# Delta-rule layer: the head-wise normalisation of the output moved from ScalarE to GpSimd

## The chip, the core and the metric

The kernel runs on one core of one Trainium2 chip. A core has five engines with queues of their own: TensorE (PE, its weight loads listed apart as PEld), VectorE (DVE), ScalarE (ACT), GpSimd (POOL) and SyncE (SP, which here only issues DMAs). They meet through semaphores alone. The metric is the device time of one execution in microseconds (us), as the median of several runs.

## The reference, cut to what matters

Two transformer-like layers over x of shape (8, 512, 128): layer 0 with attention and a capped mixture of experts, layer 1 with a gated delta rule and another mixture of experts. The change lies in the delta rule (8 batches, 512 tokens, 16 value heads, head size 64):

```python
def step(S, xs):
    q_t, k_t, v_t, g_t, b_t = xs
    S = S * jnp.exp(g_t)[..., None, None]
    kv = jnp.einsum('bhk,bhkv->bhv', k_t, S)
    S = S + jnp.einsum('bhk,bhv->bhkv', k_t, (v_t - kv) * b_t[..., None])
    o_t = jnp.einsum('bhk,bhkv->bhv', q_t, S)
    return (S, o_t)
...
var = jnp.mean(o * o, axis=-1, keepdims=True)
o = o * jax.lax.rsqrt(var + EPS) * norm_w * jax.nn.silu(z)
return o.reshape(b_, t_, V_DIM) @ W_out
```

What the change touches is the last product but one: o times its inverse norm (one number for each token and head), and then times the gate silu(z).

## The kernel before

`network` runs four stages with a barrier between them: `setup`, layer 0, `delta1` (the delta rule) and `experts1`. All that follows is in `delta1`.

**Tiling.** The recurrence is taken in chunks of CK = 32 tokens. The 8 batches are two groups of four; the four batches of a group lie side by side on the 128 partitions, 32 tokens each. Each group has NCK = 16 chunks, so there are NS = 32 steps, k = 0 to 31, with one group behind the other. Steps come in pairs m = k // 2; a step is called even or odd by k. A step works in two halves f = 0 and 1 of 8 heads (512 columns) each. Every engine has its own hand-written program, a loop over k that calls small functions, so the order on an engine is the order of the calls. Semaphore counts (`half(k, f)`, `done(kind, x)`) tie them together.

**The recurrence in a step.** TensorE reads the state (`read_out`, L2514: keys times S into the banks BK, queries times S into BQ). VectorE scales the first (`read_out`, L2010, writes Xs). GpSimd subtracts it from the values (`residual`, L1917) and decays the state (`decay`, L1929: S times GC, 128x1024, one for each half). TensorE solves the triangular system (`solve`, L2548), ScalarE copies the result (`weights`, L2319, writes Ws), GpSimd weighs it (`weigh`, L1938: Ud = Ws times dl, with dl broadcast along the head), TensorE forms the state's increment (`add_state`, L2565), and VectorE subtracts it from S (`update`, L2111). After `update(k, 1)` TensorE may do `read_out(k + 1)`.

**The output in a step.** ScalarE writes O from the bank with a decay (`decayed`, L2259), VectorE subtracts the part within the chunk (`accumulate`, L2117). In the next step ScalarE squares and sums O for each head (`square_out`, L2249, into nrm), VectorE and ScalarE turn the sums into inverse norms (`total` L2018 and L2019, `root_out` L2269, `inverse_norm` L2024 and L2025, semaphore `v_rn`). Then `normed` on ScalarE (L2326) multiplies O by nrm, head by head: 16 activations of 128x64 with a per-partition scale. `gated` on GpSimd (L1945) multiplies O by the gate zs, one instruction of 128x512 for each half. TensorE transposes O (`turned`, L2588), ScalarE copies it out (L2339), and one step later TensorE multiplies by the output weights (`output`, L2595).

**What stands behind `normed` on ScalarE.** `keys(k + 1)` copies the transposed keys to Kt (L2333), `gate(k, 0)` and `gate(k, 1)` compute zs (L2313; each waits until `gated` of the step before has read the old zs of its half), and then the copies of `turned`. TensorE's second gate product (`gate(k, 1)`, L2484) takes the bank that `keys` has to empty, and TensorE's queue is in order: behind it stand, in odd steps, the norms of keys and queries (`norms`, L2457), then `turned`, two projections (L2475), `output` and `read_out(k + 1)`.

**VectorE's fill work.** Beside the recurrence VectorE convolves (`conv`, L2057, with its sum in PSUM), builds the decay matrices in even steps (`norms` L2041 to L2047, `attend` L2071 to L2082, `turn` L2086), and inverts the triangular matrices by substitution (`substitute`, L2095 and L2096, 30 rounds of two dependent tensor_tensor instructions for each pair of steps, with all operands in SBUF). Rounds 1 to 5 stand between `update(k, 0)` and `accumulate(k, 1)` of the even step, 6 to 11 behind its `update(k, 1)`; the odd step has the rest, 18 to 23 between its two updates. The first round waits for GpSimd (`initial`, L1963 to L1968).

**GpSimd's order in a step**: `window` (copies of the layer's input), `residual` x2, `decay(k, 0)`, in even steps `diag` (L1911), `weigh` x2 and `initial`, then `decay(k, 1)`, `gated(k - 1)`, `halo`.

Of the kernel before, what the change touches and what calls it, by code (L numbers as in the profile page):

```python
# [7 lines left out]
ALU = mybir.AluOpType  # L8
ACT = mybir.ActivationFunctionType
# [23 lines left out]
HV, HK, DK = 16, 8, 64  # L33
# [1732 lines left out]
def delta1(nc, g, a, w):  # L1766
# [7 lines left out]
    with Stage(nc, ["p_ks", "p_qs", "p_w", "p_ds", "p_pu", "p_kk", "p_m",  # L1774
                    "v_ks", "a_qs", "v_s", "v_o", "v_lt", "v_at", "v_ac", "v_tt", "v_conv", "v_by", "v_ss",
                    "v_rn", "v_rk", "p_nm", "p_nt", "a_rt", "v_link", "g_x", "g_s", "g_d1", "g_t", "g_t0", "g_halo", "g_on", "g_hw", "g_ac", "v_nm", "a_kq", "g_ud",
                    "a_m", "a_w", "a_on", "a_sq", "a_osq", "a_or", "d_al0", "d_al1", "d_out",
                    "k_y0", "k_y1", "k_y2", "k_y3", "k_m", "k_x", "k_v", "k_var", "k_rstd", "k_nm", "k_xn", "k_xT", "k_hT",
                    "k_rows", "k_be", "k_e", "k_ee", "k_al", "k_alz", "k_ad", "k_ga", "k_gb", "k_gce"]) as s:
        raw = s.sb("raw", [P, 4, 2, 4, KS - 1 + 2 * CK])  # L1780
# [68 lines left out]
        with nc.Block() as block:  # L1849
# [40 lines left out]
            def _(pool):  # L1890
# [48 lines left out]
                                    ALU.mult).then_inc(s["g_ud"], 1)  # L1939

                def gated(k):
                    for f in range(2):
                        pool.wait_ge(s["a_m"], done("z", 2 * k + f))
                        pool.wait_ge(s["a_on"], half(k, f))
                        G.tensor_tensor(O[:, k % 2, f, :], O[:, k % 2, f, :], zs[:, f, :], ALU.mult)\  # L1945
                            .then_inc(s["g_on"], 1)

# [289 lines left out]
            def _(act):  # L2237
                A_ = nc.scalar.activation

                def square_out(k, f):  # L2240
                    act.wait_ge(s["v_o"], half(k, f))
                    if half(k, f) > 1:
                        act.wait_ge(s["a_osq"], half(k, f) - 1)
                    if k >= 2:
                        act.wait_ge(s["a_on"], half(k - 2, 1))
                    for h in range(HF):
                        of = slice(DK * h, DK * h + DK)
                        at = HF * f + h
                        last = A_(osq[:, of], O[:, k % 2, f, of], ACT.Square, accum_out=nrm[:, k % 2, at:at + 1])  # L2249
                    last.then_inc(s["a_osq"], 1)  # L2250
# [64 lines left out]
                def weights(k, f):  # L2315
# [1 line left out]
                    if k:  # L2317
                        act.wait_ge(s["p_pu"], half(k - 1, f))
                    A_(Ws[:, f, :], BK[f][:, :], ACT.Copy).then_inc(s["a_w"], 1)  # L2319

                def normed(k):
                    act.wait_ge(s["v_rn"], k + 1)
                    for f in range(2):
                        for h in range(HF):
                            of = O[:, k % 2, f, DK * h:DK * h + DK]
                            last = A_(of, of, ACT.Copy, scale=nrm[:, k % 2, HF * f + h:HF * f + h + 1])  # L2326
                        last.then_inc(s["a_on"], 1)

                def keys(k):
                    act.wait_ge(s["p_m"], done("kt", k))  # L2330
# [53 lines left out]
                for k in range(FIRST, LAST):  # L2384
                    here, past = 0 <= k < NS, 0 <= k - 1 < NS
                    if past:
                        square_out(k - 1, 0)
                    if (k + 4) // 2 < NP:
                        project(2 * (k + 4))
                    if k == FIRST:  # L2390
                        act.wait_ge(s["k_e"], 2)
                        A_(sy, sy, ACT.Exp).then_inc(s["k_ee"], 1)
                    if 0 <= k - 2 < NS:
                        output(k - 2)
                    if past:
                        square_out(k - 1, 1)
                    if here:
                        decayed(k, 0)
                        decayed(k, 1)
                    if here and k % 2 == 1:  # L2400
                        weights(k, 0)
                    if (k + 4) // 2 < NP:
                        project(2 * (k + 4) + 1)
                    if here and k % 2 == 0:
                        weights(k, 0)
                    if past:
                        root_out(k - 1)
                    if 0 <= k + 1 < NS:
                        values(k + 1, 0)
                    if here:  # L2410
                        weights(k, 1)
                    if (k + 4) // 2 < NP:
                        squash(2 * (k + 4))
                        squash(2 * (k + 4) + 1)
                    if k == FIRST + 1:
                        act.wait_ge(s["k_e"], 3)
                        A_(al, sp, ACT.Exp, scale=w["nA"][:, 0:1]).then_inc(s["k_al"], 1)
                    if k == -1:
                        for x in range(4):
                            last_decays(x)  # L2420
                    if 0 <= k + 1 < NS:
                        values(k + 1, 1)
                    if past:
                        normed(k - 1)
                    if 0 <= k + 1 < NS:
                        keys(k + 1)
                    if here:
                        gate(k, 0)
                        gate(k, 1)
                    if k % 2 == 1 and 0 <= k // 2 + 2 < NP:  # L2430
                        root(k // 2 + 2)
                    if past:
                        turned(k - 1, 0)
                        turned(k - 1, 1)
# [270 lines left out]
```

## Time and profile before

| | |
|---|---|
| median of 3 runs | 2621.98 us (2610.21 to 2622.99) |
| the profiled execution's own time | 2618.09 us |
| its span in the trace | 2616.3 us |
| busy, whole span | PE 2091.7, DVE 1826.4, ACT 1477.8, POOL 791.8 us |
| the 32 steps of the delta rule | from 1152.9 us to some 2190 us |
| instructions of `normed` | 512, 331 to 348 ns each |
| instructions of `gated` | 64, 1260 to 1482 ns each |
| instructions of `weigh`, 1250 to 2150 us | 54, 1038 to 1280 ns, median 1042 |

A row of a timeline is a start in us from the span's start, a duration in us, engine, line, operation, output<-inputs and a count; neighbours of one kind on one engine are merged. In brackets stands how long the engine sat idle before and what released it. An instruction's duration contains any time for which it was held up after its start. Instructions of one engine can overlap by some 0.1 us.

### The profile page before, as it was taken

What the parts mean: (1) busy time and instruction counts of PE and PEld (TensorE: products, weight loads), DVE (VectorE), ACT (ScalarE), POOL (GpSimd) and SP (SyncE); (2) the same over time, 40 slices, a digit from 0 to 9 for tenths busy, and PEclk for the clock granted to TensorE, in tenths of its full rate; (3) what the DMA queues carried; (4) which work ended last, traced back from release to release, by engine and by line L of the source; (5) the groups of instructions that cost most, each with busy time, mean ns of one, the idle gap of its engine ahead of it and who ended that gap; (6) DMA issues with size and microseconds to landing.
All of it is one profiled execution on the core that took longest, in us unless ns stands there. A gap on an engine that the chain in (4) does not pass through costs nothing. (4 is left out here: it accounts for less than half of the span.)

```text
span 2616.3 us, 64390 instructions
## 1 busy us (share of the span) xinstructions
PE 2091.7 (80%) x25432; PEld 1286.1 (49%) x25432; DVE 1826.4 (70%) x4473; ACT 1477.8 (56%) x4029; POOL 791.8 (30%) x852
## 2 busy tenths in 40 slices
PE   2698988988888584578888888888888884777984
PEld 1244444444444363245555555556555553455652
DVE  2477777777776434688899999899998863673333
ACT  0267677677676321546777777777776663222221
POOL 1000001001001134034444444444444442104884
PEclk9599999999998887788999999999999896797997
DMA  5100000000000062100000000000000003334334
GB/s 184 41 1 1 9 5 9 5 5 9 5 5 9 13 178 62 24 18 12 13 13 13 13 13 13 13 13 13 13 13 5 5 6 102 81 98 99 44 45 88
DMA packets 109533, 85.58 MB, mean 33 GB/s; under 512 B 22366, under 2 KB 97282, under 8 KB 108976
## 3 DMA queue, kind: packets, MB, share of 16 engines
q1 hardware_dynamic: 95664, 68.31, 8.9%
q0 software_dynamic: 13568, 13.14, 3.1%
q8 instruction: 202, 3.31, 0.5%
q14 instruction: 99, 0.81, 0.1%
HBM read 59.22 MB, written 22.71 MB: 31 GB/s over the span
## 5 line engine op out<-in xcount | busy, mean ns | idle before, releaser
L624 ACT ACTIVATE Pr<-Pr,nmax 128x512 f32<-128x512 f32 x512 | 341.3, 715 | 173.4 <-DVE nmax L555 170.7
L729 PE MATMUL bank<-ident,Pr 128*128 128x128 f32 x2048 | 301.5, 289 | 82.5 <-DVE PT L564 65.7
L729 PEld LDWEIGHTS bank<-ident,Pr 128*128 128x128 f32 x2048 | 231.9, 147 | 254.8 <-DVE PT L564 165.8
L555 DVE CUSTOM_DVE_ANT_0 Pr<-bank,Tb 128x512 f32<-128x512 f32 x512 | 330.9, 684 | 22.8 <-PE bank L715 20.7
L564 DVE COPY PT<-bank 128x512 f32<-128x512 f32 x256 | 176.5, 690 | 176.3 <-PE bank L743 171.7
L2491 PE MATMUL bank<-Wcv,hw 128*128 128x512 f32 x512 | 241.1, 615 | 4.3 <-ACT bank L2282 3.4
L2095 DVE TENSOR_TENSOR pr<-AC,Tc 128x30 f32<-128x30 f32 (+14 forms) x480 | 218.8, 456 | 33.1 <-POOL Tc L1968 19.3
L2096 DVE TENSOR_TENSOR Tc<-Tc,pr 128x30 f32<-128x30 f32 (+14 forms) x480 | 199.2, 415 | 16.5
L631 ACT ACTIVATE PT<-bank 128x512 f32<-128x512 f32 x256 | 150.7, 589 | 71.6 <-PE bank L743 66.8
L715 PE MATMUL bank<-kp,qp 8*128 8x512 f32 x1024 | 172.6, 663 | 0.8 <-DVE nmax L555 0.8
L1917 POOL TENSOR_TENSOR Xs<-vt,Xs 128x512 f32<-128x512 f32 x64 | 80.8, 1274 | 277.2 <-DVE Xs L2010 276.1
L433 POOL DMA_INDIRECT disp<-H,slot x32 | 31.8, 994 | 402.2 <-DVE slot L504 394.9
L2491 PEld LDWEIGHTS bank<-Wcv,hw 128*128 128x128 f32 x512 | 95.5, 194 | 108.2 <-issue 97.7
L743 PE MATMUL bank<-PT,vp 128*9 128x512 f32 x1024 | 145.8, 640 | 0.0
L2326 ACT ACTIVATE O<-O,nrm 128x64 f32<-128x64 f32 x512 | 125.3, 334 | 2.8 <-DVE nrm L2025 2.8
L2484 PE MATMUL bank<-Wz,hw 128*128 128x512 f32 x128 | 81.4, 723 | 53.6 <-ACT Kt L2333 33.3
L424 POOL TENSOR_SCALAR H<-X,rs,nm 128x128 f32<-128x128 f32 x32 | 13.9, 448 | 361.4 <-DVE nm L543 361.4
L2249 ACT ACTIVATE osq<-O 128x64 f32<-128x64 f32 x512 | 122.9, 250 | 0.0
L2057 DVE SCALAR_TENSOR_TENSOR bank<-raw,cwq,bank 128x256 f32<-128x256 f32 x256 | 111.8, 483 | 4.6 <-ACT bank L2282 1.8
L1929 POOL TENSOR_TENSOR S<-S,GC 128x1024 f32<-128x1024 f32 x60 | 115.0, 1916 | 0.0
L1596 POOL DMA_INDIRECT acc<-eo,ids x64 | 100.9, 1577 | 43.7 <-DVE eo L1731 19.9
L1945 POOL TENSOR_TENSOR O<-O,zs 128x512 f32<-128x512 f32 x64 | 82.2, 1293 | 102.2 <-ACT O L2326 102.2
(407 smaller groups left out, 4437.5 us busy)
## 6 DMA issues: line engine op xcount, KB each, us to landing
aB<-alpha SPq DMA_DIRECT2D x64, 128.0 KB, 2.8
Tb<-scores SPq DMA_DIRECT2D x1, 7168.0 KB
w<-in_L_ffn_W SPq DMA_DIRECT2D x16, 256.0 KB, 5.4
rawW<-in_L_ffn_up_w SPq DMA_DIRECT2D x16, 256.0 KB, 3.1
rawW<-in_L_ffn_gw SPq DMA_DIRECT2D x16, 256.0 KB, 3.5
rawW<-in_L_ffn_down_w SPq DMA_DIRECT2D x16, 256.0 KB, 4.0
disp<-zero SPq DMA_DIRECT2D x1, 2580.0 KB, 14.7
xin<-disp SPq DMA_DIRECT2D x8, 322.5 KB, 6.1
```

The costliest lines, as they stand in the source:

```text
L555: V.tensor_tensor_reduce(out=Pr[:, s, i, :], in0=pS[hh][:, :], in1=Tb[:, h, at:at + L], scale=-1.0, scalar=3.0e38, op0=ALU.add, op1=ALU.mi ...
L564: V.tensor_copy(PT[:, m % NPS, :], pT[m % 2][:, :]).then_inc(r["b_evd"], 1)
L624: A_(Pr[:, s, i, :], Pr[:, s, i, :], ACT.Exp, scale=-1.0, bias=nmax[:, s, i:i + 1])\
L631: A_(PT[:, m % NPS, :], pT[m % 2][:, :], ACT.Copy).then_inc(r["b_eva"], 1)
L715: mm(pS[hh][:, :], qp[rows, G % SLOTS, i * P:(i + 1) * P], kp[rows, G % SLOTS, :], start=True, stop=True, tile_position=(32 * hh, 0)).then ...
L729: last = TR(pT[m % 2][:, t * P:(t + 1) * P], Pr[:, (G % 2) * HG + hh, t, j * P:(j + 1) * P], ident[:, :])
L743: mm(pO[32 * hh:32 * hh + HD0 + 1, :], vp[:, b % 2, j, G % NG * HG + hh, :], PT[:, m % NPS, :], start=(j == 0), stop=(j == LT - 1), tile_p ...
L2095: link(V.tensor_tensor(o, bcast(AC[:, i + 1:CK, i], 2, i), bcast(Tc[:, i, 0:i], 1, n), ALU.mult))
L2096: link(V.tensor_tensor(Tc[:, i + 1:CK, 0:i], Tc[:, i + 1:CK, 0:i], o, ALU.add))
L2249: last = A_(osq[:, of], O[:, k % 2, f, of], ACT.Square, accum_out=nrm[:, k % 2, at:at + 1])
L2326: last = A_(of, of, ACT.Copy, scale=nrm[:, k % 2, HF * f + h:HF * f + h + 1])
L2491: last = mm(o[:, :], tokens(k, i), Wcv[:, i, 512 * f:512 * f + 512], start=(i == 0), stop=(i == KS - 1))
```

## The change

`normed` on ScalarE is gone, with its 16 activations a step. `gated(k)` on GpSimd first waits for the inverse norms (`v_rn`), multiplies each half of O by nrm, broadcast along the head (two instructions of 128x512), and then multiplies by the gate as before (two instructions). The semaphore `a_on` becomes `g_nrm`, which GpSimd raises; ScalarE's `square_out` waits on it where it waited on `a_on`. Nothing else is changed: VectorE's and TensorE's programs are the same.

```diff
 def gated(k):
+    pool.wait_ge(s["v_rn"], k + 1)
+    for f in range(2):
+        G.tensor_tensor(hd(O[:, k % 2, f, :]), hd(O[:, k % 2, f, :]),
+                        bcast(nrm[:, k % 2, HF * f:HF * f + HF], 2, DK), ALU.mult)\
+            .then_inc(s["g_nrm"], 1)
     for f in range(2):
         pool.wait_ge(s["a_m"], done("z", 2 * k + f))
-        pool.wait_ge(s["a_on"], half(k, f))
+        pool.wait_ge(s["g_nrm"], half(k, f))
         G.tensor_tensor(O[:, k % 2, f, :], O[:, k % 2, f, :], zs[:, f, :], ALU.mult)\
             .then_inc(s["g_on"], 1)
...
 def square_out(k, f):
...
     if k >= 2:
-        act.wait_ge(s["a_on"], half(k - 2, 1))
+        act.wait_ge(s["g_nrm"], half(k - 2, 1))
...
-def normed(k):
-    act.wait_ge(s["v_rn"], k + 1)
-    for f in range(2):
-        for h in range(HF):
-            of = O[:, k % 2, f, DK * h:DK * h + DK]
-            last = A_(of, of, ACT.Copy, scale=nrm[:, k % 2, HF * f + h:HF * f + h + 1])
-        last.then_inc(s["a_on"], 1)
...
     if 0 <= k + 1 < NS:
         values(k + 1, 1)
-    if past:
-        normed(k - 1)
     if 0 <= k + 1 < NS:
         keys(k + 1)
```

GpSimd in the last part of an even step and the first of the odd step behind it, before:

```order
L1963 TENSOR_TENSOR AC<-AC,rkT 128x1024
L1965 AFFINE_SELECT Tc<-AC 128x1024
L1968 MEMSET Tc 128x32
L1929 TENSOR_TENSOR S<-S,GC 128x1024
L1945 TENSOR_TENSOR O<-O,zs 128x512 x2
L1956 COPY raw<-raw 128x8x3 x2
L1904 COPY hw<-hTa 128x128 x4
L1917 TENSOR_TENSOR Xs<-vt,Xs 128x512 x2
```

The same place with the change:

```order
L1968 TENSOR_TENSOR AC<-AC,rkT 128x1024
L1970 AFFINE_SELECT Tc<-AC 128x1024
L1973 MEMSET Tc 128x32
L1929 TENSOR_TENSOR S<-S,GC 128x1024
L1944 TENSOR_TENSOR O<-O,nrm 128x512 x2
L1950 TENSOR_TENSOR O<-O,zs 128x512 x2
L1961 COPY raw<-raw 128x8x3 x2
L1904 COPY hw<-hTa 128x128 x4
L1917 TENSOR_TENSOR Xs<-vt,Xs 128x512 x2
```

The two products with nrm stand between the second decay of the state and the products with the gate; all else keeps its order (line numbers behind L1941 are higher by 5).

## Rows read from the trace of the kernel before

**Rows 1.** The page, part 1: busy us, share of the span, instructions.

```profile
PE 2091.7 (80%) x25432; PEld 1286.1 (49%) x25432; DVE 1826.4 (70%) x4473; ACT 1477.8 (56%) x4029; POOL 791.8 (30%) x852
```

**Rows 2.** VectorE's waits, 1250 to 2150 us: us in total, times, longest.

```profile
DVE Xs L2010 <- PE bank L2514: 28.4, 26, 3.5
...
DVE S L2111 <- PE bank L2565: 12.1, 15, 4.0
```

**Rows 3.** Busy time by stretch: length, five engines, PEclk: steps 11, 12, 25.

```profile
1514.60:1546.50 31.90, 27.11 (x437) 16.32 (x439) 28.97 (x65) 22.81 (x74) 12.91 (x14) 0.95 0.01 2
1546.50:1579.40 32.90, 30.65 (x726) 21.95 (x719) 29.43 (x59) 25.23 (x108) 17.53 (x19) 0.95 0.10 23
1966.00:2000.80 34.80, 28.72 (x434) 16.80 (x436) 31.32 (x65) 22.34 (x72) 12.70 (x14) 0.85 0.01 2
```

**Rows 4.** Group by form, 1250 to 2150 us: busy us, mean ns, idle before.

```profile
L1938 POOL TENSOR_TENSOR Ud<-Ws,dl 128x512 f32<-128x512 f32 x54 | 58.5, 1083 | 88.3 <-ACT Ws L2319 88.3
```

**Rows 5.** Timeline, last half of step 11 (odd): ACT, PE, POOL, DVE.

```profile
1530.39 3.91 ACT L2326 ACTIVATE O<-O,nrm 128x64 f32<-128x64 f32 x16
...
1534.84 1.13 PE L2484 MATMUL bank<-Wz,hw 128*128 128x512 f32 x2 [2.13 <-ACT Kt L2333]
...
1545.31 1.95 PE L2514 MATMUL bank<-S,kq 64*32 64x128 f32 x76
...
1526.71 1.90 POOL L1929 TENSOR_TENSOR S<-S,GC 128x1024 f32<-128x1024 f32 x1
1532.54 1.37 POOL L1945 TENSOR_TENSOR O<-O,zs 128x512 f32<-128x512 f32 x1 [3.93 <-ACT O L2326]
...
1528.79 0.17 DVE L2025 TENSOR_TENSOR nrm<-nrm,rkq 128x16 f32<-128x16 f32 x1
...
1529.48 1.28 DVE L2111 TENSOR_TENSOR S<-S,bank 128x512 f32<-128x512 f32 x2
...
1546.46 0.69 DVE L2010 TENSOR_TENSOR Xs<-bank,gk 128x512 f32<-128x512 f32 x1 [1.40 <-PE bank L2514]
```

**Rows 6.** Timeline, last third of step 12 (even): POOL, DVE, ACT, PE.

```profile
1566.38 1.90 POOL L1929 TENSOR_TENSOR S<-S,GC 128x1024 f32<-128x1024 f32 x1
1568.24 2.48 POOL L1945 TENSOR_TENSOR O<-O,zs 128x512 f32<-128x512 f32 x2
...
1569.60 1.20 DVE L2095 TENSOR_TENSOR pr<-AC,Tc 128x58 f32<-128x58 f32 x1
1570.83 0.25 DVE L2096 TENSOR_TENSOR Tc<-Tc,pr 128x58 f32<-128x58 f32 x1
...
1569.59 0.60 ACT L2313 ACTIVATE zs<-bank 128x512 f32<-128x512 f32 x1 [2.06 <-POOL O L1945]
...
1575.65 1.62 PE L2514 MATMUL bank<-S,kq 64*32 64x128 f32 x52
```

**Rows 7.** Timeline, start of step 12 (even), VectorE.

```profile
1547.82 0.69 DVE L2010 TENSOR_TENSOR Xs<-bank,gk 128x512 f32<-128x512 f32 x1 [0.67 <-PE bank L2514]
...
1548.52 0.19 DVE L2042 TENSOR_TENSOR gk<-gT,rkq 128x32 f32<-128x32 f32 x1
1548.62 1.26 DVE L2043 COPY rkd<-rkq 128x32 f32<-128x32 f32 x1
...
1552.92 1.22 DVE L2071 TENSOR_TENSOR_SCAN Lt<-aB,Lt 128x512 f32<-128x512 f32 x1
```

**Rows 8.** Timeline, start of step 0, VectorE.

```profile
1152.90 0.63 DVE L2010 TENSOR_TENSOR Xs<-bank,gk 128x512 f32<-128x512 f32 x1
1153.96 0.69 DVE L2010 TENSOR_TENSOR Xs<-bank,gk 128x512 f32<-128x512 f32 x1 [0.43 <-PE bank L2514]
...
1154.87 1.30 DVE L2042 TENSOR_TENSOR gk<-gT,rkq 128x32 f32<-128x32 f32 x1
1156.10 1.92 DVE L2043 COPY rkd<-rkq 128x32 f32<-128x32 f32 x1
...
1160.77 1.22 DVE L2071 TENSOR_TENSOR_SCAN Lt<-aB,Lt 128x512 f32<-128x512 f32 x1
```

More of the change, by code:

```diff
@@ L1776, in delta1 @@
                     "v_rn", "v_rk", "p_nm", "p_nt", "a_rt", "v_link", "g_x", "g_s", "g_d1", "g_t", "g_t0", "g_halo", "g_on", "g_hw", "g_ac", "v_nm", "a_kq", "g_ud",
-                    "a_m", "a_w", "a_on", "a_sq", "a_osq", "a_or", "d_al0", "d_al1", "d_out",
+                    "a_m", "a_w", "g_nrm", "a_sq", "a_osq", "a_or", "d_al0", "d_al1", "d_out",
                     "k_y0", "k_y1", "k_y2", "k_y3", "k_m", "k_x", "k_v", "k_var", "k_rstd", "k_nm", "k_xn", "k_xT", "k_hT",
```

## The prediction, made blind

> **What bounds the kernel now.** The page's first part [rows 1] shows TensorE at 80% and VectorE at 70% of the span, ScalarE at 56%, GpSimd at 30%. That speaks for moving work from ScalarE to GpSimd, but it is an average over four stages. So I cut the delta rule into steps with the table of stretches [rows 3]. An odd step (11) takes 31.9 us with VectorE busy for 29.0, the even one behind it (12) 32.9 with 29.4; ScalarE is busy for 22.8 and 25.2. The stage has 32 such steps, and a barrier behind it, so what it loses or gains shows in the total.
>
> The table of waits [rows 2] says what VectorE lacks: in 900 us (28 steps) 28.4 us for TensorE's read-out of the state and 12.1 for the state's increment, its largest waits beside that for GpSimd's first matrix, which the change doesn't touch. VectorE sets the pace, and TensorE's late read-out adds about 2 us to each pair of steps. In the timeline of step 11 [rows 5] that lateness begins at the line that the change removes: 3.91 us of `normed`, then TensorE's second gate product idle for 2.13 us until Kt is copied, and 12 us later VectorE idle for 1.40 us until the read-out. The second L2010 waits for another 0.67 us [rows 7]. So the removed work is on a path that costs something, in odd steps. In the even step the relief can't help: the read-out started at 1575.65 [rows 6], and VectorE came to it only at 1579.4 [rows 3].
>
> The third view is VectorE's own durations, and it decides. In step 12 [rows 6] L2095 with 58 columns takes 1.20 us and its partner L2096 with 58 columns 0.25 us. The first lies beside GpSimd's products with the gate (1568.24 to 1570.72), the second behind them.  So a VectorE instruction with both inputs in SBUF is held until the GpSimd instruction beside it ends. The state's update L2111, which has one input in PSUM, takes 1.28 us for two [rows 5], 0.64 each for 512 columns, with nothing added. VectorE's busy time has these holds in it.
>
> The Trainium skill ("SBUF — State Buffer", section "Who interferes with whom") states this as a rule against such a move: a VectorE instruction with two SBUF inputs contends with a GpSimd instruction that reads SBUF, one with at most one doesn't, and the loser blocks fully. The rows just named agree (1.20 against 0.25 us). Were the page's lock paid for the whole of every added instruction, wherever it lies, the result would be the second rival below.
>
> **The change part by part.** Per step, ScalarE loses 16 activations (3.91 us in step 11). GpSimd gains two broadcast products of 128x512. The nearest row is `weigh`, the same form: mean 1083 ns [rows 4], of which some 1.05 is its length when nothing holds it. Two make 2.1 us. GpSimd has room in sum (12.9 and 17.5 busy of 32 us [rows 3]), so only the place matters.
>
> *Odd steps, relief.* `keys` no longer waits behind `normed`, so TensorE's second gate product starts up to 2.13 us sooner, and all behind it (norms, transposes, projection, output, read-out). VectorE's wait of 1.40 us before the first L2010 goes. The waits for the read-out are 28.4 us; 14 of the second L2010 by 0.67 are 9.4 of these, so the first ones are 19, about 1.4 for each odd step: **-19 us**.
>
> *Odd steps, cost.* The inverse norms are ready at 1528.96 and GpSimd is free then (its decay ended at 1528.61) [rows 5]. The two new products would run to 1531.1. Beside them VectorE has `accumulate` and `update(k, 0)`, up to 1530.76 [rows 5], with their PSUM inputs, which aren't held; only the next L2095 is, for some 0.3 us. The gate products still hold two substitution instructions, as they do now. **+4 us** for 14 steps.
>
> *Even steps, end.* Here GpSimd is late: after Tc it has `decay(k, 1)` (1566.38 to 1568.28) and then the gate products back to back [rows 6]. The inverse norms were ready long before, so the new products go in between, and five GpSimd instructions in a row stand where three did. VectorE is in rounds 1 to 5, whose instructions take some 0.25 us free [rows 6], and gets one through for each GpSimd instruction. Two more are held: 2 x (1.05 - 0.25) = 1.6 us, ahead of `update(k, 1)`, on which the next step waits. 14 steps (2 to 28): **+22 us**. Nothing hides it: VectorE doesn't wait at the odd step's start.
>
> *Even steps, start.* This term is the least obvious. In step 12 the second L2010 comes 1.36 us behind the first, since the read-out is late [rows 5, 7]; L2041 and L2042 then slip between GpSimd's two `residual` instructions (0.19 us) and L2043 is held by the second (1.26). In step 0 the read-out was less late (0.43 in place of 0.67), the second L2010 came 1.06 us behind the first, and the pattern is another: L2042 held for 1.30 us by the second `residual` and L2043 for 1.92 by the decay [rows 8]. From the first L2010 to the scan L2071 step 0 needs 7.87 us, step 12 6.46; step 0 has no L2018 and L2019 (0.28 us). So a read-out that comes 0.3 us sooner costs 1.7 us. With the relief of 2.13 us against waits of 1.40 the second L2010 won't wait, and step 0's pattern becomes that of the even steps. Between 0 and 1.7 I take 1.7, since step 0 shows it, for 12 of 14 steps (behind step 15, which has no update, and at one other the read-out stays late): **+20 us**. The 0.67 us of waiting is inside this figure.
>
> *The rest.* With VectorE later, L2111's small waits in even steps go (0.2 us each): **-3**. Behind the last step `normed` and the second gate product in series are 3.9 + 1.3 = 5.2 us, four products 4.6. Steps 30 and 31, where VectorE has little to do, may gain some 1 us each: with these **-2.5**.
>
> *A cover.* In even steps zs and the transposes wait for the gate products (the 2.06 us of L2313 [rows 6]), so the new 2.1 us delay TensorE as well, and with the start's 1.7 the read-out begins some 4 us later in the step. Now it begins 3.75 us ahead of VectorE's L2010 (1575.65 against 1579.4) and needs 1.15 of these (1545.31 to 1546.46 in step 11 [rows 5]). VectorE itself is later by 3.3. Hidden, with some 2 us to spare.
>
> Sum: -19 + 4 + 22 + 20 - 3 - 2.5 = +21.5. Against the profiled execution's 2618.1 us that is 2639.6. The median of 2622 is 4 above this execution; the three runs spread over 13 us. I say **2640 us**.
>
> **The rivals.**
>
> *Relief wins (faster).* The decisive point is whether VectorE is held by the new products at the even step's end. If TensorE's and ScalarE's queues are what paces that end (zs waits 2.06 us there), or if GpSimd's products don't hold these short instructions, and the start pattern stays as in step 12, only the relief is left: -19 - 9 for the second L2010, -3, -2.5, and some for zs: 2585 us. For it: 3.9 us a step leave a queue behind which TensorE waits. Against: 1.20 against 0.25 [rows 6].
>
> *Every added instruction is paid in full (slower still).* If VectorE's phase shifts so that the new products meet substitution in odd steps too, 62 x 1.05 = 65 us of holds replace the 26 above: 2679 us. Against: the `v_rn` that releases them comes right ahead of the PSUM work in VectorE's own order.
>
> *The start pattern stays (no change).* Without the +20: 2618 + 1.5 = 2620 us. This needs the read-out to stay as late as now, for instance since the clock is lower.
>
> *The clock (slower).* Step 25 takes 34.8 us against step 11's 31.9, with the granted clock at 0.85 in place of 0.95 [rows 3]: stretches at 1.2 in place of 2.4 GHz behind idle time of TensorE. The even steps get more idle time (2 us ahead of the transposes), the odd ones less. Should a third of the odd steps more go that way: +3 x 5 = 15 on the forecast, 2655 us; the other way round, -3 x 3 = -9 on it.
>
> **How the numbers follow.** Forecast 2640: 0.5. Clock above it: 0.1. Start pattern stays: 0.22. Relief wins: 0.1. Paid in full: 0.08. The range takes in all but the relief's centre and the full price: 2606 to 2668. A measurement tells about 0.5% from no change, 13 us, so faster is below 2609, slower above 2635: faster 0.11, same 0.3 (the pattern case and the forecast's lower edge), slower 0.59.
>
> **What would show it.** Right, if in the trace after: (1) even steps last 35 to 36 us and odd ones near 31; (2) L2010's waits for the read-out in odd-to-even turns are gone; (3) L2043 takes 1.9 us in even steps, with the scan about 8.1 us behind the first L2010; (4) five GpSimd instructions in a row at the even step's end with five VectorE ones of 1 to 1.9 us beside them; (5) in odd steps the new products lie beside L2117 and L2111 of unchanged length. Wrong, if VectorE waits at the start of odd steps (TensorE has become late there, the cover is gone), if L2043 is still at 1.26 us (the start term falls), or if the substitution's mean time is as before (the holds fall).

## The result, and the profile after

| | before | after |
|---|---|---|
| median of 4 runs each | 2620.07 us (2610.21 to 2622.99) | 2644.20 us (2643.39 to 2647.32) |
| the profiled execution | 2618.09 us | 2647.32 us |
| span in the trace | 2616.3 us | 2645.5 us |

The changed kernel is slower: the ratio is 1.0107, with a 95% interval of 1.0078 to 1.0135. The forecast was 2640 us.

ScalarE has lost 116 us of busy time and GpSimd has gained 68 (against [rows 1]); VectorE, whose program is the same, has gained 54:

```profile
PE 2086.5 (79%) x25432; PEld 1296.6 (49%) x25432; DVE 1880.7 (71%) x4473; ACT 1361.8 (51%) x3517; POOL 859.9 (33%) x916
```

VectorE's waits from 1250 to 2150 us (us in total, times, longest). The read-out, 28.4 us in [rows 2], is down to 0.2:

```profile
DVE S L2116 <- PE bank L2560: 4.8, 4, 2.5
...
DVE Xs L2015 <- PE bank L2509: 0.2, 1, 0.2
```

So the wait went as forecast, and VectorE's own instructions became longer. Steps 11, 12 and 25, with the columns of [rows 3]:

```profile
1533.20:1565.10 31.90, 30.00 (x570) 19.83 (x561) 30.39 (x65) 23.76 (x87) 14.97 (x16) 1.00 0.02 4
1565.10:1601.20 36.10, 27.40 (x588) 19.22 (x591) 33.19 (x61) 16.97 (x63) 19.61 (x21) 0.91 0.07 19
2004.00:2036.10 32.10, 30.12 (x574) 19.98 (x566) 30.58 (x65) 24.13 (x90) 15.30 (x16) 1.00 0.02 6
```

The even step takes 36.1 us in place of 32.9, with 3.8 us more of VectorE. The odd step 11 takes 31.9 as before: its wait is gone, and VectorE is busy for 1.4 us longer.

**The even step's end** (step 12; GpSimd, then VectorE; to be read against [rows 6]). Five GpSimd instructions stand in a row, and beside them VectorE gets through five, one for each, of 0.98 to 1.84 us. The sixth, behind them, takes 0.27:

```profile
1586.66 1.90 POOL L1929 TENSOR_TENSOR S<-S,GC 128x1024 f32<-128x1024 f32 x1
1588.52 2.04 POOL L1944 TENSOR_TENSOR O<-O,nrm 128x512 f32<-128x512 f32 x2
1590.52 2.49 POOL L1950 TENSOR_TENSOR O<-O,zs 128x512 f32<-128x512 f32 x2
...
1586.77 1.84 DVE L2100 TENSOR_TENSOR pr<-AC,Tc 128x30 f32<-128x30 f32 x1 [1.81 <-POOL Tc L1973]
1588.64 0.98 DVE L2101 TENSOR_TENSOR Tc<-Tc,pr 128x30 f32<-128x30 f32 x1
1589.66 0.98 DVE L2100 TENSOR_TENSOR pr<-AC,Tc 128x58 f32<-128x58 f32 x1
1590.67 1.18 DVE L2101 TENSOR_TENSOR Tc<-Tc,pr 128x58 f32<-128x58 f32 x1
1591.88 1.22 DVE L2100 TENSOR_TENSOR pr<-AC,Tc 128x84 f32<-128x84 f32 x1
1593.14 0.27 DVE L2101 TENSOR_TENSOR Tc<-Tc,pr 128x84 f32<-128x84 f32 x1
```

**The even step's start** (step 12, VectorE; against [rows 7]). The pattern is now that of step 0 in [rows 8]: L2047 (L2042 of before) is held for 1.31 us and L2048 (L2043) for 1.92, and the scan starts 8.14 us behind the first L2015 (L2010), formerly 6.46:

```profile
1565.09 1.22 DVE L2015 TENSOR_TENSOR Xs<-bank,gk 128x512 f32<-128x512 f32 x2
...
1567.04 1.31 DVE L2047 TENSOR_TENSOR gk<-gT,rkq 128x32 f32<-128x32 f32 x1
1568.27 1.92 DVE L2048 COPY rkd<-rkq 128x32 f32<-128x32 f32 x1
...
1573.23 1.22 DVE L2076 TENSOR_TENSOR_SCAN Lt<-aB,Lt 128x512 f32<-128x512 f32 x1
```

**The odd step.** In step 11 (GpSimd, VectorE) the new products lie beside L2122 and L2116, which are as long as ever. But `decay(k, 1)` reaches over L2030 (L2025 of before), which takes 1.52 us where [rows 5] had 0.17:

```profile
1546.88 1.90 POOL L1929 TENSOR_TENSOR S<-S,GC 128x1024 f32<-128x1024 f32 x1
1548.89 2.04 POOL L1944 TENSOR_TENSOR O<-O,nrm 128x512 f32<-128x512 f32 x2
...
1547.30 1.52 DVE L2030 TENSOR_TENSOR nrm<-nrm,rkq 128x16 f32<-128x16 f32 x1
1548.74 0.67 DVE L2122 TENSOR_TENSOR O<-O,bank 128x512 f32<-128x512 f32 x1
1549.34 1.27 DVE L2116 TENSOR_TENSOR S<-S,bank 128x512 f32<-128x512 f32 x2
```

**Where the 29.2 us of the span come from.** A step is counted from its first L2010 or L2015 to the next step's.

| part | before | after | difference |
|---|---|---|---|
| start of the delta rule | 1152.9 | 1155.2 | +2.3 |
| step 0 | 32.0 | 39.2 | +7.2 |
| 14 even steps, 2 to 28 | 461.9 | 502.3 | +40.4 |
| 15 odd steps, 1 to 29 | 484.1 | 471.8 | -12.3 |
| from step 30 to the next stage | 63.4 | 60.7 | -2.7 |
| the last stage | 421.9 | 416.3 | -5.6 |

The first, second and last of these lie where the change touches nothing. Step 0 goes with TensorE's clock. The mean granted clock is 0.94 there before and 0.75 after (the row below). With two levels, 1.2 and 2.4 GHz, twice the missing share is the time at the lower one: 3.8 us of 32.0 before, 19.6 of 39.2 after. TensorE is busy for 36.5 us there, where before it was 27.0, and VectorE waits for it for 7.26 us at one place, where before it didn't wait:

```profile
1155.20:1194.40 39.20, 36.47 (x705) 24.24 (x698) 25.25 (x57) 18.19 (x71) 14.95 (x17) 0.75 0.07 16
...
1176.52 1.03 DVE L2083 TENSOR_TENSOR A<-bank,Lt 128x512 f32<-128x512 f32 x1 [7.26 <-PE bank L2531]
```

### The profile page after: what moved, and what is told of

It is laid out like the page before. It is cut to its first block and busy times, and to the rows that moved or that the text cites. A ratio compares the mean times of both kernels' runs of the same rounds, so it can differ in the third digit from the quotient of the medians.

```text
span 2645.5 us, 63942 instructions
## 1 busy us (share of the span) xinstructions
PE 2086.5 (79%) x25432; PEld 1296.6 (49%) x25432; DVE 1880.7 (71%) x4473; ACT 1361.8 (51%) x3517; POOL 859.9 (33%) x916
## 5 line engine op out<-in xcount | busy, mean ns | idle before, releaser
L2100 DVE TENSOR_TENSOR pr<-AC,Tc 128x30 f32<-128x30 f32 (+14 forms) x480 | 231.2, 482 | 33.8 <-POOL Tc L1973 20.0
L2486 PE MATMUL bank<-Wcv,hw 128*128 128x512 f32 x512 | 250.4, 634 | 5.7 <-ACT bank L2287 4.0
L2101 DVE TENSOR_TENSOR Tc<-Tc,pr 128x30 f32<-128x30 f32 (+14 forms) x480 | 207.1, 431 | 16.5
L2318 ACT ACTIVATE zs<-bank 128x512 f32<-128x512 f32 x64 | 38.1, 597 | 143.7 <-POOL O L1950 133.4
L2509 PE MATMUL bank<-S,kq 64*32 64x128 f32 x4096 | 109.3, 276 | 2.3 <-DVE S L2116 2.3
L2583 PE MATMUL bank<-ident,O 128*128 128x128 f32 x256 | 51.0, 345 | 74.9 <-ACT zs L2318 65.6
```

What stands on the lines that cost most here:

```text
L2100: link(V.tensor_tensor(o, bcast(AC[:, i + 1:CK, i], 2, i), bcast(Tc[:, i, 0:i], 1, n), ALU.mult))
L2101: link(V.tensor_tensor(Tc[:, i + 1:CK, 0:i], Tc[:, i + 1:CK, 0:i], o, ALU.add))
L2486: last = mm(o[:, :], tokens(k, i), Wcv[:, i, 512 * f:512 * f + 512], start=(i == 0), stop=(i == KS - 1))
```

## The experiments

In the tables "even" is the mean of steps 2 to 28 and "odd" that of steps 1 to 29, from each kernel's profile (before 32.99 and 32.27, after 35.88 and 31.45). A profile is one execution and lies up to 9 us from its kernel's median, so a total is read from the median and the steps from the profile. The ratio is to the kernel before, timed on the same chip. The names in the diffs are those of the program; lines are each kernel's own.

**The theory:** the loss is what GpSimd's products do to VectorE, at the even step's end and in the start pattern. **The rivals:** it is TensorE's or ScalarE's queue (the products delay the output path); or the relief itself sets off the costly start; or the added work costs its full length wherever it lies.

### Relief without the products, and the products without relief

The first leaves the normalisation out altogether; where the gate products and `square_out` waited for `a_on`, they wait for `v_rn`:

```diff
 def gated(k):
+    pool.wait_ge(s["v_rn"], k + 1)
...
-        pool.wait_ge(s["a_on"], half(k, f))
...
-def normed(k):
...
-                    if past:
-                        normed(k - 1)
```

> The kernel before with the normalisation left out altogether (no multiplication by nrm on any engine; the gate products wait for the inverse norms). It has the relief of ScalarE's queue without GpSimd's new products. Theory (VectorE is held by GpSimd, and the relief itself brings the costly start pattern of even steps): L2043 goes from 1.26 to 1.9 us in even steps and the scan comes 8.1 us behind the first L2010, so the relief of 19 us is eaten by 20; the gate products of odd steps move beside PSUM work, about -15; in sum some 2600 us. Rival (ScalarE's queue paces the steps and the start pattern stays): L2043 stays at 1.26 us and the time falls by 35 to 50 us, 2570 to 2585.

The second is the whole kernel before plus two products of the new form and length in the new place, whose output nothing uses:

```diff
 def gated(k):
+    pool.wait_ge(s["v_rn"], k + 1)
+    for f in range(2):
+        G.tensor_tensor(hd(scr[:, f, :]), bcast(ident[:, 0:DK], 1, HF), bcast(scn[:, :], 2, DK), ALU.mult)
```

> The kernel before with two more GpSimd products a step (a constant tile times a constant broadcast, 128x512 each, into a scratch tile) at the place where the changed kernel has its own; ScalarE keeps its 16 activations. Cost without relief. Theory: even steps' ends get the two more holds of VectorE, +22 us, odd steps little, L2043 stays at 1.26 us since the read-out is as late as before: 2640 to 2650 us, even steps about 34.6 us. Rival (holds don't count, the changed kernel is slower for another reason, such as the start pattern alone): 2620 to 2627.

| | median us | ratio (95%) | even | odd |
|---|---|---|---|---|
| relief alone | 2583.14 | 0.9875 (0.9847 to 0.9903) | 33.62 | 29.74 |
| products alone | 2639.17 | 1.0105 (1.0068 to 1.0142) | 35.27 | 31.49 |

The added products cost, by themselves, as much as the whole change. In the last third of step 10 (GpSimd, VectorE) they do what they do in the changed kernel, though nothing reads their result:

```profile
1507.00 2.04 POOL L1948 TENSOR_TENSOR scr<-ident,scn 128x512 f32<-128x512 f32 x2
...
1507.13 0.98 DVE L2103 TENSOR_TENSOR Tc<-Tc,pr 128x30 f32<-128x30 f32 x1
1508.14 0.98 DVE L2102 TENSOR_TENSOR pr<-AC,Tc 128x58 f32<-128x58 f32 x1
```

The two parts don't add up: -31 us (against the median of 2614.45 for the kernel before, timed beside them) and +25, but +24 when both are done. The waits of this second kernel from 1250 to 2150 us show why:

```profile
DVE Xs L2017 <- PE bank L2521: 7.9, 8, 3.6
```

The wait for the read-out, 28.4 us in [rows 2], is down to 7.9 without any relief, for VectorE itself comes later. With the products in place the relief finds little left to relieve.

The run also corrects the theory. I expected L2043 to stay at 1.26 us and even steps of about 34.6 us. In seven of the 14 even steps the scan comes 8.14 or 8.15 us behind the first read: VectorE, held up at the even step's end, finds the read-out ready, and the second read waits less or not at all. So two causes, relief and holds, lead to the same costly start. The relief alone brings it in only six of the 14 steps (8, 10, 12, 14, 22, 26; in step 8 L2043 takes 1.93 us); in six others the scan comes as early as 6.34 us. That is why relief alone gave 31 us, near the 33 of the rival "relief wins", and not the 0 of my two terms (-19 and +20). Its 2583 us lie in the range that I had given the rival (2570 to 2585), not at the 2600 of the theory.

What parts the two forms shows in steps 4 and 8 of this kernel, each with its second `residual` product and L2042:

```profile
1279.54 1.32 POOL L1917 TENSOR_TENSOR Xs<-vt,Xs 128x512 f32<-128x512 f32 x1
1279.55 0.18 DVE L2042 TENSOR_TENSOR gk<-gT,rkq 128x32 f32<-128x32 f32 x1
...
1405.19 1.27 POOL L1917 TENSOR_TENSOR Xs<-vt,Xs 128x512 f32<-128x512 f32 x1
1405.20 1.31 DVE L2042 TENSOR_TENSOR gk<-gT,rkq 128x32 f32<-128x32 f32 x1
```

In both the second read doesn't wait and L2042 starts some 0.01 us behind the product. In step 8 it is held; in step 4 it isn't, and the product takes 0.05 us more. Over all the kernels whose `norms` stand in this place, L2042's counterpart was held in every step in which it started 0.013 us or more behind the product, and in no step in which it started ahead of it; at 0.006 to 0.012 us both came. With relief alone it mostly lies at 0.006 to 0.012, in steps 4 to 26 of the changed kernel at 0.017 to 0.027. So an absent wait for the second read makes the costly start possible, and about 0.01 us decides. What sets these hundredths isn't shown.

### The same products at half their length

The output's columns 256 to 511 of each half aren't multiplied by nrm.

```diff
-        G.tensor_tensor(hd(O[:, k % 2, f, :]), hd(O[:, k % 2, f, :]),
-                        bcast(nrm[:, k % 2, HF * f:HF * f + HF], 2, DK), ALU.mult)\
+        G.tensor_tensor(hd(O[:, k % 2, f, 0:256]), hd(O[:, k % 2, f, 0:256]),
+                        bcast(nrm[:, k % 2, HF * f:HF * f + HF // 2], 2, DK), ALU.mult)\
```

> The changed kernel with GpSimd's two new products over 256 of the 512 columns of each half only (the other heads stay without normalisation). Each new hold is shorter by 0.5 us, and so is the delay of the gate products, for which zs and TensorE's transposes wait. Theory: even steps lose 2 x 0.45 us from the holds and 35.1 us is left; in odd steps TensorE is late by 1 us less, so the second decay of the state ends sooner and L2030 is held for 0.3 to 0.5 us instead of 1.4: odd steps about 31.1; 2644 - 14 x (0.9 + 0.8) = 2620. Rival (only the number of GpSimd instructions counts, not their length): 2638 to 2646.

It took 2616.15 us, ratio 0.9991 (0.9969 to 1.0013), even 34.87, odd 30.70. With the count of instructions the same and only their length halved, the loss is gone from the total, as forecast:

```profile
1566.00 1.18 POOL L1944 TENSOR_TENSOR O<-O,nrm 128x256 f32<-128x256 f32 x2
```

So it hangs on GpSimd's time (two in 1.18 us for 2.04), not on the queue entries, the semaphores or the order. The even steps still take 1.88 us more than before, most of it the costly start, which 11 of 14 have. The odd steps gain 0.75 us each. In the mean of the nine ordinary ones (5 to 13 and 17 to 23) the step is 0.87 us shorter than in the changed kernel: L2030 takes 0.97 us for 1.31, and the substitution is 0.53 us shorter in sum.

Both this kernel and the one with the products alone shift the output path together with GpSimd's time. That the even step is set by VectorE's holds, and not by the queues behind that path, rests on VectorE's own rows: in the changed kernel it hardly waits for TensorE (from 1250 to 2150 us 0.2 us for the read-out and 4.8 for the increment), and it is busy for 3.8 us more in an even step that is 3.2 us longer.

### Moving what collides

Two changes of order in the changed kernel, alone and together; the computation stays whole. First, VectorE does its small `norms` instructions behind a `conv` instead of beside `residual` and the decay:

```diff
-                    if ahead and e == 0:
+                    if ahead and e == 0 and k == -2:
                         norms(m + 1)
...
                         conv(2 * (k + 4))
+                    if ahead and e == 0 and k != -2:
+                        norms(m + 1)
```

> The changed kernel with VectorE's norms (its L2046 to L2052) behind the first convolution of the even step instead of ahead of it, so that the convolution, whose sums are in PSUM, lies beside GpSimd's residual products and decay. Theory: the start term of 1.7 us for each even step goes almost whole (scan about 6.6 us behind the first L2015), -18 to -22 us, 2622 to 2626. Rival (the start's holds are time in which VectorE would have waited anyway): 2640 to 2646.

Second, GpSimd does its four output products of the even step before `initial`, while VectorE works from PSUM (`conv`) or waits:

```diff
+                    if e == 0 and 0 <= k - 1 < NS:
+                        gated(k - 1)
                     if ahead:
                         initial(m + 1)
...
-                    if 0 <= k - 1 < NS:
+                    if e == 1 and 0 <= k - 1 < NS:
                         gated(k - 1)
```

> The changed kernel with gated(k-1) in even steps ahead of initial instead of behind decay(k, 1): GpSimd does the four products while it would wait for VectorE's matrix. Theory: the four holds at the even step's end go (2 x 0.8 + 2 x 0.95 = 3.5 us), initial starts some 0.5 us later and one scan may be held for 1 us: about -2 us for each of 14 steps, 2610 to 2622. Rival (GpSimd's holds at the end don't set the pace): no change beyond 5 us, 2639 to 2649, or slower, since initial is later.

> The changed kernel with both moves: norms behind the first convolution in even steps, and gated(k-1) ahead of initial in even steps. Alone they gave 7 and 16 us. Theory (both are holds of VectorE in the even step, the gain is partly given back in odd steps where TensorE is then late): even steps 33.1 us, odd ones 32.5 to 34, together 2615 to 2627 us. Rival (the gains add in full and odd steps go back to 31.0): 2600 to 2610.

| | median us | ratio (95%) | even | odd |
|---|---|---|---|---|
| norms behind conv | 2636.99 | 1.0080 (1.0055 to 1.0105) | 35.27 | 31.49 |
| gate products early | 2628.26 | 1.0039 (1.0014 to 1.0063) | 33.32 | 32.89 |
| both | 2617.31 | 1.0007 (0.9985 to 1.0028) | 33.08 | 32.45 |

Moving `norms` gave 7 us where I expected some 20, and the intervals of the two ratios overlap; in the profiles the even steps are 0.61 us shorter each. L2048 fell to 0.17 us, but VectorE reached the scan earlier, beside `weigh`, and there a scan whose 1.22 us is its free length took 2.05 (step 12, GpSimd, VectorE):

```profile
1559.71 1.04 POOL L1938 TENSOR_TENSOR Ud<-Ws,dl 128x512 f32<-128x512 f32 x1
...
1558.38 0.17 DVE L2048 COPY rkd<-rkq 128x32 f32<-128x32 f32 x1
...
1559.78 2.05 DVE L2076 TENSOR_TENSOR_SCAN Lt<-aB,Lt 128x512 f32<-128x512 f32 x1
```

Moving the gate products gave 16 us where I expected 22 to 34. It takes the holds off the even step's end, where after the first L2102 the rounds run at 0.22 to 0.30 us each (step 12, VectorE), and the even steps fall by 2.56 us, though nine of them still have the costly start:

```profile
1585.01 1.84 DVE L2102 TENSOR_TENSOR pr<-AC,Tc 128x30 f32<-128x30 f32 x1 [2.84 <-POOL Tc L1973]
...
1587.20 0.22 DVE L2102 TENSOR_TENSOR pr<-AC,Tc 128x58 f32<-128x58 f32 x1
```

The odd steps give back 1.44 us each, which I hadn't expected. Step 11 (its stretch, TensorE, VectorE) shows how: eight matmuls for values at its start take 5.25 us, where the changed kernel has 3.59 for the same eight, with a granted clock of 0.91 over the step against 1.00, and VectorE waits for the increment:

```profile
1528.08:1562.10 34.02, 32.46 (x550) 20.80 (x542) 30.04 (x65) 22.23 (x78) 14.88 (x16) 0.91 0.01 2
...
1531.04 5.25 PE L2488 MATMUL bank<-Wcv,hw 128*128 128x512 f32 x8
...
1545.58 1.28 DVE L2118 TENSOR_TENSOR S<-S,bank 128x512 f32<-128x512 f32 x2 [2.46 <-PE bank L2562]
```

Together the two moves bring the changed kernel back to the time of the kernel before, by order alone, with the steps that I expected (33.1, and 32.5 to 34). The profiled executions of "gate products early" and "both" lie 23 us apart, the medians 11; 7 us of the 23 are step 0, which is 38.8 us in the one and 31.6 in the other.

### Half by half

Is TensorE's lateness at the even step's end harmless, as my "cover" had it? This kernel finishes one half (nrm, then gate) before the other, so that zs and the transposes of the first half start sooner:

```diff
         G.tensor_tensor(... nrm ..., ALU.mult)\
             .then_inc(s["g_nrm"], 1)
-    for f in range(2):
         pool.wait_ge(s["a_m"], done("z", 2 * k + f))
```

> The changed kernel with GpSimd's products taken half by half (nrm, gate, nrm, gate in place of nrm, nrm, gate, gate). The same instructions and holds; the first half is ready 1.05 us sooner, the second at the same time. Theory (VectorE's holds set the loss, the read-out waits on the second half): 2640 to 2646, no change. Rival (TensorE's wait for zs sets the loss): 5 to 15 us faster, 2630 to 2639.

It took 2653.24 us, ratio 1.0128 (1.0088 to 1.0168), even 35.85, odd 32.09. Neither expectation held, though the interval overlaps the changed kernel's (1.0078 to 1.0135). The even steps are the same length; the odd ones are 0.64 us longer. In step 12 the order of the halves frees the first gate earlier but the second later (GpSimd; then ScalarE's two zs, of which the second starts 28.53 us into the step, against 28.01 in the changed kernel), and what follows needs the second:

```profile
1585.72 1.04 POOL L1944 TENSOR_TENSOR O<-O,nrm 128x512 f32<-128x512 f32 x1
1586.90 1.30 POOL L1949 TENSOR_TENSOR O<-O,zs 128x512 f32<-128x512 f32 x1
1588.16 1.04 POOL L1944 TENSOR_TENSOR O<-O,nrm 128x512 f32<-128x512 f32 x1
1589.34 1.36 POOL L1949 TENSOR_TENSOR O<-O,zs 128x512 f32<-128x512 f32 x1
...
1588.29 0.60 ACT L2317 ACTIVATE zs<-bank 128x512 f32<-128x512 f32 x1 [6.53 <-POOL O L1949]
1590.79 0.60 ACT L2317 ACTIVATE zs<-bank 128x512 f32<-128x512 f32 x1 [1.90 <-POOL O L1949]
```

So a gate that is later by half a microsecond, with GpSimd's work otherwise the same, leaves the even step as it was and costs in the next odd one. There VectorE now waits for TensorE, which it didn't in the changed kernel (waits from 1250 to 2150 us, 4.8 and 0.2 there):

```profile
DVE S L2115 <- PE bank L2559: 10.1, 13, 2.5
DVE Xs L2014 <- PE bank L2508: 6.5, 16, 0.6
```

The counterpart of L2030 is hardly held here (0.29 us in the mean of the nine ordinary odd steps, against 1.31), so TensorE's lateness costs by more than one way. Each gate product here starts about 0.14 us behind the end of the product that it waits for, so the two causes of the later gate (the order, and these gaps) aren't told apart.

### ScalarE's order alone

If the harm of `normed` is that `keys` stands behind it, it needn't go, only step aside. The kernel before, with all its work:

```diff
-                    if past:
+                    if past and k % 2 == 0:
                         normed(k - 1)
                     if 0 <= k + 1 < NS:
                         keys(k + 1)
+                    if past and k % 2 == 1:
+                        normed(k - 1)
```

> The kernel before with keys(k+1) ahead of normed(k-1) in ScalarE's odd steps: TensorE's second gate product no longer waits for the 16 activations, which stay on ScalarE. Relief without any new work on GpSimd. Theory: the 1.4 us wait of VectorE at the even step's start goes, the costly start pattern comes in some even steps: 2620 - 19 + 0 to 20, 2600 to 2618. Rival (the wait only moves to the read-out's other inputs, ScalarE's copies of the transposes): 2618 to 2624.

It took 2606.43 us, ratio 0.9957 (0.9934 to 0.9980), even 33.76, odd 31.66: faster than both kernels. In step 11 (ScalarE, TensorE) Kt is copied ahead of the 16 activations, and TensorE's second gate product starts with no wait, where [rows 5] had 2.13 us:

```profile
1525.21 0.59 ACT L2333 ACTIVATE Kt<-bank 128x512 f32<-128x512 f32 x1
1525.68 3.92 ACT L2326 ACTIVATE O<-O,nrm 128x64 f32<-128x64 f32 x16
...
1527.45 1.13 PE L2486 MATMUL bank<-Wz,hw 128*128 128x512 f32 x2
```

Ordinary odd steps come down to 30.5 us (9, 11, 21, 25), which is the relief that I had forecast for the change. In seven even steps the costly start takes some of it back (a scan 8.14 us behind the first read), and steps 13, 17, 19 and 27 take 33.4 to 34.7 us at a granted clock of 0.80 to 0.90.

Adding the move of VectorE's `norms`, here ahead of the read of the state in even steps, evened out the even steps at 33.28 but gave no further gain that can be told:

> The kernel e8 (ScalarE's keys ahead of normed in odd steps) with VectorE's norms of even steps ahead of the first L2010, while GpSimd is idle, so that none of its instructions is held. Theory: they cost 0.75 us ahead of L2010 and the scan comes 6.4 us behind it in every even step, so even steps take 33.5 us in place of e8's mean of 33.8, and none 34.6: 2600 to 2606 us. Rival (the start pattern isn't worth its place): 2608 to 2620, since 0.75 us is added to the path of the recurrence.

It took 2610.32 us, ratio 0.9977 (0.9954 to 1.0000), odd 31.32. I had expected 2600 to 2606; the total lies in the rival's range (2608 to 2620), while the even steps came out as the theory had them (33.5, none at 34.6).

### GpSimd only where it is free

In odd steps GpSimd multiplies by nrm, as in the change; in even steps ScalarE does, as before. Nothing is left out.

```diff
 def gated(k):
+    if k % 2 == 0:
+        pool.wait_ge(s["v_rn"], k + 1)
...
-                    if past:
+                    if past and k % 2 == 0:
                         normed(k - 1)
```

> The change in odd steps only: there GpSimd multiplies by nrm (beside VectorE's PSUM work), in even steps ScalarE keeps its 16 activations (there TensorE hardly waits for them). Theory: odd steps get the relief, and L2030's counterpart is held less than in the changed kernel, since TensorE isn't delayed by the even step's end: odd steps 30.5 to 31; even ones 33.0 or 34.6, by the start pattern: 2595 to 2610 us. Rival (every added GpSimd product costs its length wherever it lies): 2630 to 2640.

It took 2617.31 us, ratio 0.9993 (0.9976 to 1.0009), even 33.96, odd 31.58. The expectation of 2595 to 2610 failed. The ordinary odd steps are what I had forecast for the change, 30.6 to 31.1 us, with L2034 (L2025 of before) mostly at 0.17 to 0.37. But steps 5, 9, 13 and 21 take 33.5 to 35.0 at a granted clock of 0.85 to 0.90 (1.00 in the ordinary ones), and eight even steps have the costly start at 34.6.

## Why the prediction was right, and where not

**VectorE is held at the even step's end: right, and at its price.** Behind the start pattern the even step has 27.95 us left (36.10 less 8.15) where it had 26.50 (32.97 less 6.47): +1.45 a step, with the small waits for the increment (12.1 to 4.8 us) inside. The terms of +22 and -3 gave 1.4 a step. Read off the instructions, the substitution is 1.47 us longer in sum, in the mean of steps 4 to 14 and 18 to 26, for the 1.6 of the forecast. The products alone and the half length show that it is GpSimd's time that does it. The Trainium skill ("SBUF — State Buffer", "Who interferes with whom") says that the loser of the shared port blocks for the other's whole instruction; the five VectorE instructions of 0.98 to 1.84 us beside five of GpSimd agree with it, and L2122 and L2116, with an input in PSUM, at 0.67 and 0.64 us beside the new products, do too. The row that the prediction gave for this last point, L2111 at 1529.48 [rows 5], doesn't show it: GpSimd stood idle from 1528.61 to 1532.54. And the prediction's short form (at most one SBUF input, no hold) leaves out the exception that the section makes for two-port modes; L2048, a copy with one input, is held for 1.92 us.

**The even step's start: right in size, incomplete in cause.** It costs 1.68 us (8.14 less 6.46) in 12 of 14 steps, as forecast. The cause that the prediction named, the relief, brings it in only six steps by itself. The other is VectorE's own lateness, as the products alone show. The prediction took the whole 1.7 us because step 0 shows it; the two forms lie about 0.01 us apart, so that it came in all 12 steps of the changed kernel was in part luck. The rival "the start pattern stays" would have been wrong even had there been no relief.

**The even steps together:** 40.4 us against a forecast of 39 (22 + 20 - 3).

**The odd steps: the sum right, its make-up wrong.** I forecast -19 + 4 = -15; they gave -12.3. But the nine ordinary ones (5 to 13 and 17 to 23) gained 0.2 us in all. The 1.40 us of waiting went as forecast, and L2030's 1.35 us of hold and 0.3 of the next L2100 took its place. What did gain was steps 3, 25 and 27 (35.1, 34.8 and 34.5 us to 30.9, 32.1 and 32.1), from which the lower clock had gone (step 25: 0.85 to 1.00), with 9.3 us, of which 5.9 are the waits for the read-out that the relief had counted; and step 15, which has no update behind it, with 2.5. So the term that was mis-sized is the **+4 for the odd steps' cost**: 0.3 us a step forecast, and in step 11 1.5 measured (1.40 of wait gone, and the step 0.13 longer); over the nine, whose waits before were 1.14 in the mean, 1.1. There L2030 alone grew from 0.36 to 1.31 us in the mean, and the substitution by 0.24 in sum. A slip in the relief is too small to matter: the 26 waits of [rows 2] are 13 of each read, not 14, so the first reads' share is 19.7 us, not 19.

**Why: the cover.** The prediction saw that the read-out would come some 4 us later in the even step, and called that "hidden, with some 2 us to spare". It was hidden from VectorE's read: TensorE (step 12, below) starts the read-out 1.95 us before VectorE comes to it at 1601.17, formerly 3.75. But it wasn't hidden from what TensorE does next.

```profile
1592.52 2.34 PE L2583 MATMUL bank<-ident,O 128*128 128x128 f32 x8 [5.26 <-ACT zs L2318]
1594.65 1.91 PE L2470 MATMUL bank<-hTa,Wqk 128*128 128x256 f32 x4
1596.36 2.93 PE L2590 MATMUL bank<-Wo,OT 128*128 128x128 f32 x16
1599.22 2.55 PE L2509 MATMUL bank<-S,kq 64*32 64x128 f32 x100
```

TensorE idles for 5.26 us until zs, which waits for the gate products, and what stands behind it runs at 1.2 GHz up to 1598.41: L2583, L2470 and part of L2590. Its queue is in order, so it enters the odd step late: in step 11 the solve L2543 starts 5.60 us behind the first L2015 (1538.80 less 1533.20), where before it was 3.95 us behind L2010 (1518.55 less 1514.60). Ws, `weigh` and the decay follow some 1.6 us later in the step (the decay at 13.68 for 12.11), and the decay, which ended ahead of L2025 before, now lies over L2030. The solve's row after:

```profile
1538.80 2.04 PE L2543 MATMUL bank<-Xs,Tt 32*32 32x64 f32 x128
```

and before:

```profile
1518.55 2.04 PE L2548 MATMUL bank<-Xs,Tt 32*32 32x64 f32 x128
```

My "what would show it wrong" had named TensorE late at the start of odd steps with VectorE waiting there. TensorE was late, but the price came as a hold on an instruction of 0.17 us in mid-step. In the changed kernel this hold is most of the price (0.95 of 1.1 us). With TensorE earlier or later the odd steps follow (half length 0.75 shorter, half by half 0.64 longer), but by other ways as well: the half length takes 0.34 us off L2030 and 0.53 off the substitution, and half by half the price comes as waits for TensorE, as that sign had it, with L2030's counterpart almost free. The solve starts 4.31 us behind the first read before, 5.47 in the changed kernel, 5.16 at half length and 6.35 half by half, in the mean of the nine. So the odd steps go with TensorE's lateness, and the way by which it costs changes from kernel to kernel. Half by half comes nearest to a run that shifts the lateness alone; none does it cleanly.

**The clock: a rival that came in both directions.** The prediction gave it +3 for each odd step that would go that way. It left the odd steps and moved to the even ones (step 12: 0.95 to 0.91), where TensorE idles longest ahead of the transposes. Twice the missing share: step 11 had 3.2 us at 1.2 GHz and now has none, step 12 had 3.3 and now has 6.5. In the even steps it seems to cost little: they take the same 36.1 us at 0.86 (step 4) and at 0.91 (step 12). Step 0 is 7.2 us longer with it, in a stretch that the change doesn't touch.

**So the total was right in part by balance and luck.** 40.4 - 12.3 - 2.7 = +25.4 for the parts that the prediction spoke of, against +21.5; and +3.9 from elsewhere (2.3 + 7.2 - 5.6). The three executions without a profile agree with the profiled one to 4 us; whether they have step 0's stretch too can't be seen.

**The rivals.** "Relief wins" fell with the products alone; its 2585 is what the relief by itself gives (2583). "Paid in full" fell: with +29 against +61. "Start pattern stays" fell with the 1.92 us of L2048.

## What to carry to other kernels

Before work moves to an idle engine, look at which instructions of the engine that sets the pace it will lie beside, and with which operands. Here 2 us a step on an engine that was busy for 30% of the span took back all that came of removing 4 us a step from another, and 24 us more. Try the queue's own order first: putting one copy ahead of sixteen gave 0.4% where moving the sixteen lost 1.1%. A lateness that is hidden from its first reader is to be followed one step further, to whatever it sets next to what.

## What the runs showed of the hardware that I had not expected

Whether an instruction is held is decided by about 0.01 us, and the price comes in fixed sizes. The same three instructions at the even step's start put the scan at 6.34, 6.47 or 8.15 us behind the first read, in neighbouring steps of one execution (the kernel with GpSimd in odd steps only has all three). Very small instructions are held as long as large ones: 16 elements a partition took 1.52 us in place of 0.17, and the 32-element copy 1.92.

A scan with both inputs in SBUF is held too, but paid in part: 2.05 us for 1.22, with 0.97 us of a product left when it started.

Time at 1.2 GHz isn't a fixed share of the kernel. It moved from the odd steps to the even ones when TensorE's idle time did, and step 0 took 39.2, 38.8 and 37.9 us in three of the kernels' profiles and 32.0 to 32.1 in six others with the same code there. What decides step 0 stays open.
